# Neighbourhood attention's values written from SBUF straight into their gathered form

## The reference

```python
qkv = (x @ w_qkv.T + b_qkv).reshape(B, H, W, 3, h, d)
q, kk, v = qkv[..., 0, :, :] * d ** (-0.5), qkv[..., 1, :, :], qkv[..., 2, :, :]
si = jnp.clip(jnp.arange(H) - k // 2, 0, H - k)     # first row of each pixel's window; sj likewise
kw, vw = win(kk), win(v)                            # (B, H, W, 7, 7, h, d)
attn = softmax(einsum('bijhd,bijpqhd->bijhpq', q, kw) + bias)
out = einsum('bijhpq,bijpqhd->bijhd', attn, vw).reshape(B, H, W, C) @ w_p.T + b_p
```

## Time and profile before

| | |
|---|---|
| median of three runs | 3133.16 us |
| the profiled execution's time | 3134.44 us |
| its span, first to last instruction | 3132.4 us |
| TensorE busy | 2877.5 us (92%) |
| VectorE, ScalarE, GpSimd busy | 62%, 46%, 34% |
| DMA queue of SyncE (q1) | 401248 packets, 199.32 MB, 29.1% of 16 engines |
| DMA queue of ScalarE (q10) | 17868 packets, 10.19 MB, 1.7% |
| na_windows<-na_values on SyncE | 160 of 113.8 KB, 32 of 81.2 KB |
| na_values<-na_vo_na on ScalarE | 32 of 260.0 KB |
| na_v_na<-na_windows on SyncE | 128 of 390.0 KB, 128 of 16.2 KB |

### The profile page before, as it was taken

One profiled execution on the slowest core, in us unless ns is written; L12 is line 12 of the kernel. 1 busy time (PEld: TensorE's weight loads), 2 busy tenths in 40 slices (PEclk: granted clock), 3 DMA queues, 4 the chain that ended last, 5 costly groups with the idle time before them and its releaser, 6 DMA issues. The chain is left out here.

```text
span 3132.4 us, 61484 instructions
## 1 busy us (share of the span) xinstructions
PE 2877.5 (92%) x23047; PEld 2223.5 (71%) x23047; DVE 1936.2 (62%) x3839; ACT 1436.2 (46%) x3076; POOL 1073.7 (34%) x1108
## 2 busy tenths in 40 slices
PE   5989999589987889999999999999779998999799
PEld 4667777334442558888988988888558887888455
DVE  5555558558846446666666666666457776776465
ACT  2545555321135325555555555555436665667200
POOL 3444445049923035555555555554100000000100
PEclk9999999789989799999999999999879999999899
DMA  7988784000003333444343443433200000000000
GB/s 165 176 175 169 171 172 129 1 14 1 1 3 118 141 66 80 86 85 88 79 88 81 89 88 80 89 81 65 65 7 1 1 1 1 1 1 1 10 22 31
DMA packets 419407, 213.44 MB, mean 68 GB/s; under 512 B 326260, under 2 KB 398604, under 8 KB 417324
## 3 DMA queue, kind: packets, MB, share of 16 engines
q1 hardware_dynamic: 401248, 199.32, 29.1%
q10 hardware_dynamic: 17868, 10.19, 1.7%
HBM read 177.82 MB, written 52.89 MB: 74 GB/s over the span
## 5 line engine op out<-in xcount | busy, mean ns | idle before, releaser
L1795 DVE TENSOR_TENSOR sl_vl_slot<-sl_psV_slot,sl_vh_slot 128x512 fp32r<-128x512 f32 x1024 | 636.1, 684 | 381.1 <-ACT sl_vh_slot L1777 380.8
L1777 ACT ACTIVATE sl_vh_slot<-sl_psV_slot 128x512 fp32r<-128x512 f32 x1024 | 529.5, 605 | 512.4 <-PE sl_psV_slot L1732 511.0
L1750 PE MATMUL sl_psY_slot<-sl_vl_slot,sp_Mh_sp 64*128 64x512 f32 x2048 | 417.2, 389 | 0.8 <-DVE sl_vl_slot L1795 0.3
L1750 PE MATMUL sl_psY_slot<-sl_vh_slot,sp_Ml_sp 64*128 64x512 f32 x2048 | 414.5, 386 | 0.0
L1750 PE MATMUL sl_psY_slot<-sl_vh_slot,sp_Mh_sp 64*128 64x512 f32 x2048 | 414.4, 386 | 0.0
L1708 POOL TENSOR_TENSOR sl_fl_slot<-sl_f_slot,sl_fh_slot 128x512 fp32r<-128x512 f32 x256 | 336.8, 1315 | 20.5
L1706 POOL CAST sl_fh_slot<-sl_f_slot 128x512 fp32r<-128x512 f32 x256 | 166.4, 650 | 451.2 <-PE sl_psV_slot L1732 450.0
L2191 DVE TENSOR_TENSOR ca_ptl_ca<-ca_psT_ca,ca_pth_ca 128x512 fp32r<-128x512 f32 (+1 forms) x272 | 183.8, 676 | 168.4 <-ACT ca_pth_ca L2128 168.3
L2128 ACT ACTIVATE ca_pth_ca<-ca_psT_ca 128x512 fp32r<-128x512 f32 (+1 forms) x272 | 158.8, 584 | 183.2 <-PE ca_psO_ca L87 179.2
L1750 PEld LDWEIGHTS sl_psY_slot<-sl_vl_slot,sp_Mh_sp 64*128 64x128 f32 x2048 | 207.8, 184 | 38.0 <-issue 12.7
L2255 POOL TENSOR_TENSOR ex_pick_ex<-ident 128x8 fp32r<-128x8 f32 x1 | 0.2, 203 | 665.0 <-POOLq L70 665.0
(11 more groups left out here) (397 smaller groups left out, 6260.6 us busy)
## 6 DMA issues: line engine op xcount, KB each, us to landing
sl_f_slot<-filt_hat SPq DMA_DIRECT2D x1024, 64.0 KB, 2.2
na_v_na<-na_windows SPq DMA_DIRECT2D x128, 390.0 KB
na_windows<-na_values SPq DMA_DIRECT2D x160, 113.8 KB, 7.9
na_values<-na_vo_na ACTq DMA_DIRECT2D x32, 260.0 KB, 9.0
u_hat<-fw_o_fwd SPq DMA_DIRECT2D x8, 1024.0 KB, 3.8
sl_u_slot<-u_hat SPq DMA_DIRECT2D x128, 64.0 KB, 2.2
y_hat<-sl_y_slot SPq DMA_DIRECT2D x128, 64.0 KB, 1.8
X<-in_x SPq DMA_DIRECT2D x8, 512.0 KB, 7.8
```

The costliest lines, as they stand in the source:

```text
L1750: mm = e.matmul(psY[half][:, :], left[pl][rows, :], right[pr][rows], start=kc == 0 and k == 0 and x == 0 and z == 0, stop=kc == KC - 1 and ...
L1777: e.activation(v_out(0, n, q), bank(4 * n + q), ACT.Copy).then_inc(S["v_high"], 1)
L1795: e.tensor_tensor(v_out(1, n, q), bank(m), v_out(0, n, q), ALU.subtract).then_inc(S["v_split"], 1)
```

## The change

The store to na_values is gone, and so is that tensor. SyncE writes each piece u from v_out straight into na_windows as soon as VectorE has made it. A piece is 4 times 128 pixels, j = 0 to 3, and 128 pixels are two image rows, h = 0 and 1; partition p holds pixel p of each of the four, so a DMA takes 14 partitions at a step of four, each with its four pixels j of 130 numbers, and so writes the four image rows 2j + h. That makes for each piece two times ten DMAs and two times two for the border squares, 24 a piece, again in three thirds. v_out has eight buffers, one for each piece, and VectorE waits for the last pass's writes out of a buffer before it fills it. In the first pass pieces 0 and 1 stand ahead of the loads of steps 0 to 4, and pieces 2 to 7, whole, between these and the load of step 5; in the later ones the third of piece u stands at step_slot(24n + 3u + 1) + 5 and the two steps after it.

```diff
--- before.py
+++ after.py
@@ -178,10 +178,9 @@
-    NQ, NS, NP, NV, NO = 3, 3, 2, 5, 4
+    NQ, NS, NP, NV = 3, 3, 2, 5
...
-    PARTS = 4
-    PROWS = H // PARTS
+    GROUPED = 16 * 2 * (WIN + 2)
@@ -211,7 +210,7 @@
-        v_out = [sb(f"na_vo{i}", [128, TPC, VW]) for i in range(NO)]
+        v_out = [sb(f"na_vo{i}", [128, TPC, VW]) for i in range(NCH)]
@@ -233,8 +232,7 @@
-                            "k_in_psum", "v_in_psum", "q_in_psum", "k_out", "v_out", "q_out", ("v_stored", NO),
-                            ("v_grouped", PARTS), ("v_loaded", NV), "q_masked", "s_in_psum", "s_biased", "s_max", "s_shifted", "p_done",
+                            "k_in_psum", "v_in_psum", "q_in_psum", "k_out", "v_out", "q_out", ("v_grouped", NCH), ("v_loaded", NV), "q_masked", "s_in_psum", "s_biased", "s_max", "s_shifted", "p_done",
@@ -252,26 +250,24 @@
-                def group(n, part, third):
+                def windows(n, u, third):
                     if third == 0:
-                        for i in (n * NCH + 2 * part, n * NCH + 2 * part + 1):
-                            e.wait_ge(S["v_stored"][i % NO], 16 * (i // NO + 1))
-                    rows = slice(part * PROWS, (part + 1) * PROWS)
-                    V = T["v_dram"][n].rearrange("(r c) d -> r c d", c=W)[rows]
-                    windows = T["v_windows"][n, rows]
-                    for k in range(4 * third, min(4 * third + 4, WIN)):
-                        first = QS - KW // 2 + k
-                        e.dma_start(windows[:, k, 1:SUB - 1, :], V[:, first:first + QS * (SUB - 3) + 1:QS, :])\
-                            .then_inc(S["v_grouped"][part], 16)
-                    if third == 2:
-                        e.dma_start(windows[:, :, 0, :], V[:, 0:WIN, :]).then_inc(S["v_grouped"][part], 16)
-                        e.dma_start(windows[:, :, SUB - 1, :], V[:, W - WIN:W, :]).then_inc(S["v_grouped"][part], 16)
+                        e.wait_ge(S["v_out"], n * NCH + u + 1)
+                    rows = T["v_windows"][n, 8 * u:8 * u + 8].rearrange("(j h) k s d -> h k s j d", h=2)
+                    for h in range(2):
+                        for k in range(4 * third, min(4 * third + 4, WIN)):
+                            first = h * W + QS - KW // 2 + k
+                            e.dma_start(rows[h, k, 1:SUB - 1], v_out[u][first:first + QS * (SUB - 3) + 1:QS, :, :])\
+                                .then_inc(S["v_grouped"][u], 16)
+                        if third == 2:
+                            e.dma_start(rows[h, :, 0], v_out[u][h * W:h * W + WIN, :, :]).then_inc(S["v_grouped"][u], 16)
+                            e.dma_start(rows[h, :, SUB - 1], v_out[u][(h + 1) * W - WIN:(h + 1) * W, :, :]).then_inc(S["v_grouped"][u], 16)
...
                 def load(g):
...
                     k0 = start_of(r)
-                    for part in range((k0 + WIN - 1) // PROWS + 1):
-                        e.wait_ge(S["v_grouped"][part], 16 * (WIN + 2) * (n + 1))
+                    for u in range((k0 + WIN - 1) // 8 + 1):
+                        e.wait_ge(S["v_grouped"][u], GROUPED * (n + 1))
@@ -290,21 +286,21 @@
-                for third in range(3):
-                    group(0, 0, third)
+                for u in range(2):
+                    for third in range(3):
+                        windows(0, u, third)
                 for g in range(NV):
                     load(g)
-                for third in range(3):
-                    group(0, 1, third)
+                for u in range(2, NCH):
+                    for third in range(3):
+                        windows(0, u, third)
...
                     load(g)
-                    if NV <= g < NV + 6:
-                        group(0, 2 + (g - NV) // 3, (g - NV) % 3)
                     for n in range(1, len(PASSES)):
-                        for part in range(PARTS):
-                            third = g - step_slot(n * STEPS + 6 * part + 5) - 4
+                        for u in range(NCH):
+                            third = g - step_slot(n * STEPS + 3 * u + 1) - 5
                             if 0 <= third < 3:
-                                group(n, part, third)
+                                windows(n, u, third)
@@ -459,13 +455,6 @@
                         op.then_inc(S["q_out"], 1)
-                        store(n, u)
-
-                def store(n, u):
-                    i = n * NCH + u
-                    e.wait_ge(S["v_out"], i + 1)
-                    e.dma_start(T["v_dram"][n, u * CH:(u + 1) * CH, :].rearrange("(j p) c -> p j c", p=128),
-                                v_out[i % NO][:, :, :]).then_inc(S["v_stored"][i % NO], 16)
@@ -543,9 +532,9 @@
                     at = n * NCH + u
                     e.wait_ge(S["v_in_psum"], at + 1)
-                    if at >= NO:
-                        e.wait_ge(S["v_stored"][at % NO], 16 * (at // NO))
-                    e.tensor_tensor(v_out[at % NO][:, :, 0:128], bank_of(m)[:, :].rearrange("p (j c) -> p j c", j=TPC),
+                    if n >= 1:
+                        e.wait_ge(S["v_grouped"][u], GROUPED * n)
+                    e.tensor_tensor(v_out[u][:, :, 0:128], bank_of(m)[:, :].rearrange("p (j c) -> p j c", j=TPC),
@@ -621,7 +610,7 @@
-                for i in range(NO):
+                for i in range(NCH):
@@ -2458,7 +2447,6 @@
-    T["v_dram"] = dram("na_values", (2 * B, L, VW))
```

## The result

The changed kernel takes 3436.43 us (median of four runs, 3434.38 to 3439.28) against 3132.59 for the one before: 1.0968 times the time, 95% interval 1.0954 to 1.0983. It is slower by 304 us; 82 were forecast, and the upper end of the range, 3310, is passed by 126.

A forecast was written before the change was run, and what follows sets the result against it. TensorE, busy nine tenths of the attention's first 560 us, was taken as the bound, SyncE not. First pass +49.6 and passes +32.6 made 82.2 us on 3134.4, 3216.6, stated as 3216; range 3140 to 3310.

The forecast's parts named there:

- d: Issue time of one 14-partition window DMA, SBUF to HBM, behind another on SyncE's queue: taken as 0.51 us, ends 0.36 and 0.65.
- the nearest kind: The later y_hat store, SBUF to HBM on SyncE: shortest 0.359 us, four in a row 0.51 us each with the gap.
- The mechanism: In the attention, value products wait for loads queued behind 768 window DMAs on SyncE's queue, in program order: 82.2 us slower.
- the first pass: Attention up to step 10: pieces 2 to 7 queued ahead of load 5 make TensorE stand nearly 60 us; +49.6 us.
- the passes: Next three attention passes: SyncE needs 5.08 us per window step, TensorE 3.86; each pass stalls 17.9 us, together +32.6 us.
- its lead: SyncE running four steps ahead in the passes: 15.4 us, less 4.0 for the load's issue and landing, leaves 11.4 us.
- The undisturbed pass: One 32-step attention pass without disturbance: 24 steps at 3.86 us and 8 at 3.06, 117.1 us; three passes lost 21 us.
- Rival (b): Window DMAs cost what the old windows cost, 0.58 to 0.65 us or beyond: 3324 us at 0.65; chance 0.16.
- Rival (a): Small window DMAs issue as the loads do, 0.36 to 0.44 us: kernel 3134 to 3162 us; chance 0.21.
- Rival (c): Relief of the DMA engines decides, ending late loads at pass changes and in the first pass: 3104 us; chance 0.07.
- The clock: TensorE's clock after the long stall: a step becomes at most 4.7 us, under SyncE's 5.08, so hidden.
- The new wait of VectorE: VectorE's wait for v_grouped before overwriting v_out[u], 25 steps behind its copy except in pass 1: costs nothing.

The follow-up runs named there:

- step_one: Changed kernel with window DMAs reading 14 neighbouring partitions instead of 14 at a step of four (wrong pixels carried): 3188.17 us, ratio 1.023 to the kernel before.
- spread_all: Kernel before with window copies spread two a step instead of four, including groups 2 and 3 of the first pass: 3103.75 us, ratio 0.9953.
- interleave: Changed kernel with first-pass pieces 3 to 7 issued a third a step behind the loads of steps 5 to 19: 3436.2 us, ratio 1.1029 to the kernel before.
- sixteen2: Changed kernel with window DMAs of 16 partitions at a step of four, no border DMAs (partly wrong pixels): 3271.39 us, ratio 1.0495 to the kernel before.

## Why the prediction was wrong

**The term that failed is d**, the issue time of one window DMA, in "I take d = 0.51; the ends are 0.36 and 0.65". It was 0.82 for the 20 inner DMAs of a piece and 0.766 as the mean of 24, outside both ends. I chose the y_hat store as "the nearest kind" because direction and dimensions were alike, and did not list the one property in which no DMA of the trace was alike: a step between partitions. An operation that the trace does not show was bounded by rows that all lacked what makes it dear. The upper end should have stood open.

**The mechanism held, step by step.** Put d = 0.766 into the forecast's own sum: load 5 landed at 38.4 + 36.8 + 3.0 + 3.8 + 110.3 + 4.0 = 196.3, step 5 at 197.4 (199.0 measured), step 10 at 216.7 (219.3). A step with windows takes SyncE 7.13 us, the stall is 24 x 3.27 - 11.4 = 67 and a pass 184.2 (190.7, 191.6 and 188.1). Together 98.8 + 180.2 = 279 of 299 us. It holds away from this point as well, to about the same amount: with the 0.44 us that each of the 144 DMAs before load 5 took in step_one, the sum puts step 127 at 583, and 609.1 was measured.

**The missing 20** are 2.6 us in the first pass and 17.8 in the passes. For the 8 steps behind the last windows of a pass I had 3.06 us each, 24.5 in all. In the first two passes they fall among the next pass's steps with projections and took 30.9 us, 6.4 more; in the third no next pass is projected, and they took 25.9, 1.4 more: 14.2 together. The other 3.6 are two differences that nearly cancel. A step with windows took SyncE 7.25 to 7.34 us and not 7.13 (11 us more in three passes), and its lead was worth 13.4 to 14.8 us and not 11.4 (8 less).

**The undisturbed pass** of 117.1 us is misread for the third: 15 of its 32 steps, and not 8, have no projections, so it is 17 x 3.86 + 15 x 3.06 = 111.5, and spread_all has 111.8. The three passes of the kernel before thus lost some 27 us and not 21. That is not where the forecast failed, since in the changed kernel SyncE sets the pace of these steps.

**Where I split the sum into "the first pass" and "the passes"**, the numbers agree but the reading does not: interleave shows that the first term can be taken away and that all but 8 us of it return in the next. From 222 to 372 us, through the first pass's steps with windows, SyncE waits for nothing; in the whole attention it waits 79.8 us for value products (139.1 before). So there is in the main one term, the sum of its issues.

**Rival (b)** had the right sign of the error and the right cause in part (the number counts: 0.83 for 14 against 0.64 for 16, both stepped; that it is because 14 does not divide evenly was not tested), but ended at 0.65. **Rival (a)**, that small DMAs issue like loads, is what step_one shows for neighbouring partitions (0.42); had the layout allowed that, the kernel would still have been 2% slower: step_one is 71 us over, where the sum of (a) gave 28 for d = 0.44. **Rival (c)**'s late loads exist and can be had back, worth 0.5% in spread_all, without the change; but they go there with the DMA engines as busy as before, so that relieving the engines is what helps is not shown. The Trainium skill's rule (DMA: Bandwidth & Descriptors, Issuing engines are not separate DMA queues) that the time to initiate a DMA is usually small against the DMA itself does not carry over to this kernel: in sixteen2 windows land in 2.2 us at the median and are issued one every 0.64, in a chain where only the latter adds up.

**The clock** was hidden, as forecast: 0.84 from 230 to 350 us, with TensorE busy for 78.09 of the 120 us, so that a step's work was still shorter than SyncE's. The new wait of VectorE appears nowhere among its waits, and the eight buffers cost nothing in the kernel before.

## What to carry to other kernels

Before a transfer is cut into smaller ones, multiply their number by the issue time on their queue and compare that with the time of the loop that they must keep up with; a queue in program order also delays everything put behind it, here the loads. When an operation has a property that no row of the trace has, leave that end of the range open or look for it first, however alike the rest is. And a long stall near the start may be only the first instalment: ask what the queue would do if the stall were moved.

## What the hardware showed beyond that

- A DMA whose SBUF side steps over partitions (2, 3, 4 or 8, store or load) was issued in 0.82 to 0.85 us in a chain, one of as many neighbouring partitions in 0.42.
- With a step, the number mattered: 0.61 to 0.64 for 16, 32 and 64 partitions, 0.68 for 8, 0.78 to 0.83 for 7, 10, 12 and 14. Without one, 10 took 0.37, 14 took 0.42, 16 and 32 took 0.45, and 128 with one row each 0.46.
- With 14 stepped partitions the number of pieces hardly did: 14 pieces 0.78, 56 pieces 0.83 us.
- With the DMA engines full, issues of 260 KB without a step went from 0.405 to 0.879 us within one chain of eight.
- Why a step costs this was not found; the profile shows the duration of the issue and nothing inside it.
